# Three edits in a fused attention and feed-forward kernel: shifts of four heads turned at once, local values by tokens, reciprocals in PSUM

## The reference, cut to what matters

```
q, k, v = split_heads(x @ Wq), split_heads(x @ Wk), split_heads(x @ Wv)
# compressed branch: softmax over 32 blocks of 16 tokens (keys k_c, values v_c)
# selected branch: the 4 best blocks of each query, softmax over their 64 tokens
logits_s = where(allowed, einsum('bhtd,bhtnd->bhtn', q, k_s) / scale, NEG)
out_s = einsum('bhtn,bhtnd->bhtd', softmax(logits_s), v_s)
# local branch: the 33 last tokens of each query
wmask = (abs(pos[:, None] - pos[None, :]) <= WIN // 2) & (pos[:, None] >= pos[None, :])
out_l = einsum('bhts,bhsd->bhtd', softmax(where(wmask, q @ k.T / scale, NEG)), v)
out = gates[..., 0:1] * merge(out_c) + gates[..., 1:2] * merge(out_s) + gates[..., 2:3] * merge(out_l)
return out @ Wo
```

## Time and profile before

| | |
|---|---|
| time, median of 3 runs | 1504.34 us (1503.79 to 1508.48) |
| the profiled execution: its time | 1504.73 us |
| the profiled execution: its span, first to last instruction | 1503.0 us |
| TensorE busy | 1404.7 us (93%) |
| VectorE busy | 1213.4 us (81%) |
| ScalarE busy | 928.7 us (62%) |
| GpSimd busy | 918.6 us (61%) |
| mean granted clock of TensorE | 0.980 of full |

### The profile page before, as it was taken

How to read it: one execution, slowest core, us unless ns; L and a number is a source line. 1 busy time by engine, 2 the same in 40 slices (tenths; PEclk the granted TensorE clock), 3 DMA queues, 4 the chain that set the end, 5 groups by cost and what they waited for, 6 DMA issues and landing times. The chain is left out here.

```text
span 1503.0 us, 43856 instructions
## 1 busy us (share of the span) xinstructions
PE 1404.7 (93%) x14864; PEld 1045.2 (70%) x14960; DVE 1213.4 (81%) x4544; ACT 928.7 (62%) x1684; POOL 918.6 (61%) x845
## 2 busy tenths in 40 slices
PE   6899579999999999999999999999999999999978
PEld 4566437777777777777777777777777777777667
DVE  5545288888888889888888899999888888888812
ACT  3766336666666666666666666666666666666641
POOL 5655346666666666666666666666666666666620
PEclk8999869999999999999999999999999999999989
DMA  6556942221111222222111121222222222222027
GB/s 189 202 184 211 277 71 53 52 49 45 47 46 47 51 51 51 51 51 48 47 46 47 47 51 48 48 50 51 51 51 51 51 51 51 65 51 53 9 87 243
DMA packets 217147, 113.74 MB, mean 76 GB/s; under 512 B 128872, under 2 KB 211224, under 8 KB 217112
## 3 DMA queue, kind: packets, MB, share of 16 engines
q1 hardware_dynamic: 216304, 112.88, 27.5%
q10 hardware_dynamic: 808, 0.42, 0.2%
HBM read 73.08 MB, written 40.16 MB: 75 GB/s over the span
## 5 line engine op out<-in xcount | busy, mean ns | idle before, releaser
L1150 POOL TENSOR_TENSOR sumxy<-xy 128x1024 f32<-128x1024 f32 x128 | 240.7, 1900 | 0.0
L1393 DVE TENSOR_REDUCE bmax<-q_bank 128x32 f32<-128x512 f32 (+3 forms) x512 | 220.5, 483 | 19.9 <-PE q_bank L1633 19.7
L1240 ACT ACTIVATE pts<-k_bank 128x512 f32<-128x512 f32 (+2 forms) x384 | 177.7, 491 | 42.2 <-PE k_bank L1668 41.6
L1494 DVE SCALAR_TENSOR_TENSOR mw<-sumxy,c,ex 128x1024 f32<-128x1024 f32 x128 | 175.9, 1393 | 1.8 <-issue 1.0
L1633 PE MATMUL q_bank<-ko,qo 96*128 96x512 bf16 (+3 forms) x512 | 143.4, 307 | 26.0 <-DVE bmax L1393 24.7
L1116 POOL TENSOR_TENSOR pad<-pad 128x1 f32<-128x1 f32 x32 | 6.2, 194 | 256.5 <-DVE top L1412 256.5
L1615 PE MATMUL f_bank<-xt,wfu 128*128 128x128 f32 x1024 | 162.3, 281 | 0.0
L1174 POOL TENSOR_TENSOR cw<-cw,mw 128x1024 f32<-128x1024 f32 x64 | 150.8, 2357 | 8.1 <-ACT mw L1264 3.3
L1615 PE MATMUL f_bank<-xt,wfg 128*128 128x128 f32 x1024 | 150.5, 279 | 0.7 <-issue 0.7
L1615 PEld LDWEIGHTS f_bank<-xt,wfu 128*128 128x128 f32 x1024 | 139.4, 191 | 11.6
L1264 ACT ACTIVATE mw<-mw,erec 128x1024 f32<-128x1024 f32 x128 | 145.8, 1139 | 0.0
(11 more groups left out here) (211 smaller groups left out, 3373.6 us busy)
## 6 DMA issues: line engine op xcount, KB each, us to landing
qo<-s_qs SPq DMA_DIRECT2D x192, 64.0 KB, 2.2
ko<-s_ks SPq DMA_DIRECT2D x186, 64.0 KB, 2.2
s_qs<-parts SPq DMA_DIRECT2D x8, 768.0 KB, 4.9
s_ks<-parts SPq DMA_DIRECT2D x8, 768.0 KB, 6.3
s_v<-vo SPq DMA_DIRECT2D x8, 544.0 KB, 3.0
vv<-s_v SPq DMA_DIRECT2D x32, 136.0 KB, 2.3
vw<-s_v SPq DMA_DIRECT2D x64, 68.0 KB, 2.5
xin<-in_L_attn_x_dram SPq DMA_DIRECT2D x8, 512.0 KB, 7.2
```

The costliest lines, as they stand in the source:

```text
L1150: done("sum_done", g_.tensor_tensor(sumxy[:, h, :, :], xy[:, 0, h, 0:XK, None].broadcast_to([P, XK, KEYS]), xy[:, 1, h, None, :].broadcast ...
L1240: last = s.activation(pts[:, h, OFFS[j]:OFFS[j] + n], bank[:, 0:n], ACT.Exp)
L1393: last = v.tensor_reduce(bmax[:, i, h, 0:n], Q.bank(job)[:, o:o + n * BLK].rearrange("p (n j) -> p n j", j=BLK), AX.X, ALU.max)
L1494: done("mw_done", v.scalar_tensor_tensor(mw[:, h, :], sumxy[:, h, :, :].rearrange("p a b -> p (a b)"), c8[:, h, 7:8], ex[:, h % 2, :], ALU ...
```

## The change

1. **Shifts.** The rows for the shifts are no longer 96 to 127 of every head but rows 32h to 32h+31 of head h; the pair of parts that stood there stands in rows 96 to 127. So one `head_shifts(n)` turns all four heads with four matmuls (128 x 128 weights) into one K bank, job "a", and ScalarE copies it in four pieces of 32 rows. It runs inside the tail of step t, for n, between `token_values` and `experts_down(t, 1)`, and needs `shift_lo` and `shift_top` of n there. `queries` and `window` use all 128 rows, so the shift rows of `qo` must be zero until then: each load of parts first loads zeros there from a zero tensor in memory. With heads laid out differently, the loads of parts are 16 for keys and 16 + 4 for queries instead of 6 and 6. The lead gets the same, with the one-hot rows of `ko` copied by ScalarE's queue of transfers instead of GpSimd.
2. **Local values.** `local_values` swaps its operands: `pT` is the stationary one, and the output has tokens on the rows, 17 columns per tile and head. The transposition back (`tl`) and ScalarE's copy for it are gone. It is moved from step position (2,3) to behind `window(n)`, in two halves with the last part of mlp_down between them (which waits for the first half, `vl_half`). VectorE's `normalize(t, 1)` moves behind `local_scores(n)` and `selected_max(n)`.
3. **Reciprocals.** They are written back to the PSUM bank, so that the product with the gate has one operand in PSUM.
4. **Order on VectorE:** `expert_sum(t)` stands ahead of `key_marks(n)`.
5. **Last phase:** the first batch's `s_y` rows are loaded during the unit phase (`yr0`), and batch 1 waits only for its `ar` on TensorE.

```
-            k_jobs = ["pcT", "co", "a0"]
+            k_jobs = ["pcT", "co"]
             for h in range(HG):
-                k_jobs += [f"s{h}0", f"s{h}1", f"s{h}2"] + [f"a{h + 1}"] * (h < HG - 1) + [("pl0", "pl1", "vl", "tl")[h]]
-            k_jobs += ["vs", "ts"]
+                k_jobs += [f"s{h}0", f"s{h}1", f"s{h}2"] + [f"pl{h}"] * (h < 2)
+            k_jobs += ["vl", "vs", "ts", "a"]
...
+            PARTS = ((0, 0), (2, 0)), ((0, 1), (0, 2)), ((1, 0), (1, 1))
+            def part_rows(to, src, which, half):
+                for i, pair in enumerate(PARTS):
+                    lots = [(3, i, i + 1)] + [(i, h0, h1) for h0, h1 in ((0, i), (i + 1, HG)) if h0 < h1]
+                    for quad, h0, h1 in lots:
+                        for n in range(2):
+                            o = 32 * quad + D * n
+                            yield to[o:o + D, half, h0:h1, :], src[pair[n][which]][:, h0:h1, :]
...
-                    pairs = [(to[D * n:D * n + D, half, :, :], src[r])
-                             for to, src, parts in ((qo, q, Q_ROWS), (ko, k, K_ROWS))[:2 if keys else 1] for n, r in enumerate(parts)]
+                    pairs = [(qo[32 * h:32 * h + 32, half, h, :], s_zero) for h in range(HG)]
+                    pairs += part_rows(qo, q, 0, half)
+                    if keys:
+                        pairs += part_rows(ko, k, 1, half)
...
+                def head_shifts(t):            # ScalarE, at the end of step and lead
+                    K.wait_full(act, t, "a")
+                    for h in range(HG):
+                        rows = slice(32 * h, 32 * h + 32)
+                        last = s.activation(qo[rows, t.half, h, :], K.bank("a")[rows, :], ACT.Copy)
+                    K.released("a", last)
...
-                    cf.link(v.reciprocal(rs[:, :, :], bank[:, :, :, D]))
-                    cf.link(v.tensor_tensor(fs[:, :, :], rs[:, :, :],
+                    cf.link(v.reciprocal(bank[:, :, D], bank[:, :, D]))
+                    cf.link(v.tensor_tensor(fs[:, :, :], bank[:, :, D].rearrange("p (i h) -> p i h", i=TT),
...
+                def local_values(t, r):
+                    bank = K.bank("vl")
+                    rows = slice(64 * r, 64 * r + 64)
+                    for k in range(2):
+                        for g in range(T // 32):
+                            i, q = divmod(g, 4)
+                            o = VW * (HG * i + 2 * r + k)
+                            last = mm(bank[32 * q:32 * q + 32, o:o + VW], pT[rows, k, 32 * g:32 * g + 32],
+                                      vw[rows, t.half, g, VW * k:VW * k + VW], start=True, stop=True, skip_group_check=True)
...
+                def head_shifts(t):            # TensorE
+                    need(pe, "shift_lo", t)
+                    need(pe, "shift_top", t)
+                    K.wait_free(pe, t, "a")
                     for i in range(TT):
-                        last = mm(K.bank(f"a{h}")[SP3:P, P * i:P * i + P], shift_s[:, i, h, :], identb[:, :],
-                                  start=True, stop=True)
+                        last = mm(K.bank("a")[:, P * i:P * i + P], shift_s[:, i, :, :].rearrange("p h n -> p (h n)"),
+                                  identb[:, :], start=True, stop=True)
...
                     if n:
                         window(n, 0)
                         window(n, 1)
+                    local_values(t, 0)
+                    mlp_down(t, 3)
+                    local_values(t, 1)
                     selected_values(t)
                     transposed_weights(t)
                     experts_down(t, 0)
-                    token_values(t, 0)
+                    token_values(t)
+                    if n:
+                        head_shifts(n)
                     experts_down(t, 1)
```

More of the change, by code:

```diff
@@ L879, in build @@
         projecting.close()
+        sb, _, _ = make(outer)
+        yr0 = sb("yr0", [P, TT, C])
         inner = ExitStack()
@@ L1338, in step @@
                     shifts_and_blocks(t)
-                    openings(t)
+                    tanh(t, "g0", hidden(0), "th_done")
                     share(t, 2)
@@ L1572, in step @@
                             block_max(n, 1, part)
+                    expert_sum(t)
+                    if n:
                         key_marks(n)
@@ L1577, in step @@
                             block_max(n, 2, part)
-                    expert_sum(t)
                     if n:
@@ L1586, in step @@
                         block_shares(n)
-                    normalize(t, 1)
                     if n:
@@ L1693, in local_ready @@
                         K.wait_read(pe, t, f"pl{k}")
-                def local_values(t):
+                def local_values(t, r):
                     bank = K.bank("vl")
-                    for g in range(T // 32):
-                        for h in range(HG):
-                            rows, k = slice(64 * (h // 2), 64 * (h // 2) + 64), h % 2
-                            last = mm(bank[32 * h:32 * h + VW, 32 * g:32 * g + 32], vw[rows, t.half, g, VW * k:VW * k + VW],
-                                      pT[rows, k, 32 * g:32 * g + 32], start=True, stop=True, skip_group_check=True)
-                    K.filled("vl", last)
+                    rows = slice(64 * r, 64 * r + 64)
[5 more added lines that the diff above has]
+                                      vw[rows, t.half, g, VW * k:VW * k + VW], start=True, stop=True, skip_group_check=True)
+                    if r == 0:
+                        done("vl_half", last)
+                    else:
+                        K.filled("vl", last)
                 def local_shares(t, k):
@@ L1763, in mlp_down @@
                     for f in (2 * part, 2 * part + 1):
+                        if f == FT - 1:
+                            need(pe, "vl_half", t)
                         mm(Y.bank("y")[:, 0:C], hT[:, f, :], wfd[:, f, :], start=(f == 0), stop=False)
@@ L1790, in lead @@
                     window(n, 1)
-                    pe.wait_ge(key_blocks, 1)
+                    head_shifts(n)
                 def step(t):
@@ L1807, in step @@
                     up_rows(t, "g", 0, 1)
-                    head_shifts(t, 0)
                     up_rows(t, "g", 0, 2)
@@ L1845, in build @@
             ar = [ar0] + [sb(f"ar{b}", [P, TT, C]) for b in range(1, B)]
-            yr = [sb(f"yr{b}", [P, TT, C]) for b in range(B)]
+            yr = [yr0] + [sb(f"yr{b}", [P, TT, C]) for b in range(1, B)]
             aT = sb("aT", [P, 2, 2, T])
```

118 lines of the change are left out of this document (53 added, 65 removed).

## The result

The new kernel takes 1514.98 us (median of 4 runs, 1513.39 to 1520.06) against 1504.95 for the one before (4 runs, 1503.79 to 1508.48): a ratio of 1.0066, 95% interval 1.0041 to 1.0091. It is slower by two thirds of a per cent. The forecast was 1490.1 us, faster; the time lies inside the range (1473 to 1520) and on the other side of no change.

What follows compares the result with a forecast made beforehand. TensorE was taken as the bound, VectorE close behind; after the change GpSimd's chain would set the period at 38.45 us. From 1504.73: +2.5 - 12.3 - 1.8 - 2.6 = -14.2, so 1490.5, median 1490.1 us; range 1473 to 1520.

Steps and rivals of the forecast that it cites:

- What is late next: Section following GpSimd's chain round through the turning to the next step: period 38.45 us against 38.86, 12.3 us gained in 30.
- less 1.32 and 0.44 and plus 0.16 that is 35.49: TensorE's arrival at experts_down(t, 1), 37.09 us into the step, less head turnings and transposition, plus a local_values gap.
- 0.36 added for longer waits: TensorE's waits on block_max, 0.54 us a unit, grow by 0.36 at the last head, so it arrives at 35.85.
- TensorE's own work: Changes to turnings, transposition and local_values on TensorE sum to -1.25 us a unit, with nothing waiting.
- the two gaps of 0.16: Behind each half of local_values, a 0.16 us gap for draining the array; two instead of one.
- The chain of GpSimd: Third mw at 4.37 us, VectorE 16.30, handover 0.16, GpSimd 15.44 to shift_lo, then TensorE: period 38.45.
- Reciprocals: VectorE's product with the gate falls from 1.46 to about 0.2 us, but this gains nothing since yo waits for TensorE.
- Loads: SP's 36 loads of parts at pitch 0.466 land at 18.95 us, needed at 20.07: 1.1 us to spare.
- The lead: Turning shifts before w0 and more query transfers start step 1 at 255.4 instead of 252.93: +2.5 us.
- Last step and last phase: The last step saves 1.8 us, and the shorter wait for yr of batch 1 saves 2.6.
- The rivals named: TensorE decides, 1474.5 (0.17); SP's load queue, 1513 at pitch 0.52 (0.24); longer chain, 1499 to 1502 (0.13); local values, 1511 (0.05).
- the price of local values: Rival: local_values on TensorE at the upper end, +1.2 us a unit, of which waits cover 0.5: 1511; chance 0.05.

Runs made afterwards that it cites:

- at 40.8 and 37.2: Periods of two kernels: the new kernel with edit 4 undone, 1568.36 us, and the one with unsel on ScalarE, result_in late, zeros and mlp_down early, 1458.15 us.
- K1: The new kernel with unsel computed by ScalarE instead of VectorE: 1480.42 us, ratio 0.9845 to the kernel before.
- K5: K1 plus result_in late, zeros early, mlp_down parts 0 and 1 early, and block_shares late, added one by one: 1446.26 us, ratio 0.9606 to the kernel before.

## Why the prediction was wrong

**The step that failed** is TensorE's arrival at the turning in "What is late next": "less 1.32 and 0.44 and plus 0.16 that is 35.49", with 0.36 added for longer waits, 35.85. Measured 36.91. The sum takes work out of a whole step as if TensorE decided all of it. In the new kernel it decides only behind the window; ahead of it VectorE does, at 27.27 whether the turnings are there or not. What was taken out there (turnings 1.32, local values and the transposition 2.0, part 3 of mlp_down 1.1) is 4.4 us, and the window starts only 2.7 earlier (27.27 against 29.96): most of the rest turned into waits, on `block_max` 1.5 instead of 0.54, and 0.56 for `hT`, together 1.5 us more, where 0.36 was taken. And what was put behind it counts in full: 11.64 us to the next step instead of 8.86. So the unit comes out as long as before. That edit 2 moves work across the last wait was never priced; local values were priced for their size alone.

**A second price missed** is `unsel`. Edit 4 lets GpSimd's sums start 2.3 us earlier, and then they run under it: 1.97 instead of 0.42. The prediction priced contention with GpSimd for one product only, and did not ask which VectorE instruction the earlier sums would now meet. By the Trainium skill (SBUF — State Buffer, Who interferes with whom), not only a VectorE instruction with two inputs in SBUF contends with GpSimd: a `tensor_scalar`, as `unsel` is, can do so too when it runs in a 2-port mode. The trace agrees in the times (1.97 us under the sums, 0.42 without them); no view shows the mode. What it costs is known only in part: moving `unsel` from under the sums takes 0.23 us off the period, giving it to ScalarE takes 1.0 off, and other lengths change with either.

**Point by point.** TensorE's own work: -1.25 forecast, -1.26 measured, and that it fits to a hundredth is luck. Local values take 0.66 and 0.70, near the 1.4 taken, but the two gaps of 0.16 are not in the timeline, and the turning takes 0.22 instead of 0.35; with these the sum would be -1.7. Against it, the four parts of mlp_down take 0.3 more in the new order, and some matmul records are missing in both traces. The chain of GpSimd: third `mw` at +4.22 (4.37), `xy_in` to +20.5 (20.67), 15.60 on GpSimd (15.44), `shift_lo` at +36.2 (36.3): right to 0.2, but not what decides in the new kernel. It does in others: at 40.8 and 37.2, and with `unsel` earlier or on ScalarE. VectorE's wait ahead of `best_pairs` is gone and it waits ahead of `yo`: right. Reciprocals, worth nothing: right; the 0.2 for the product had no row behind it, and it took 0.17 us. Loads: no wait in the 28 units of the new kernel, some 1.1 to 1.5 us to spare against 1.1, though the pitch over all 36 is 0.486 and not 0.466: they land 1.7 us after issue instead of 2.2, and the unit is longer than forecast. Right by little: in step 1 TensorE does wait 1.33 us for them, and it waits in nearly every unit where local values stand in their old place. The lead: +2.5 forecast, step 1 starts 8.7 later. Of the 6.2 missed, 3.9 are there at the first load of the unit phase already (188.63 against 184.69); in the thirteen kernels with edit 1 that load comes at 184.7 to 188.8, in the three without it at 183.8 to 184.9, so most of the 3.9 is scatter between executions, and how much is edit 1's stays open. From that load to `w0` of step 0 it is 7.1 us more, where 6.1 was forecast: queries wait 4.5 us for `ko`, and 0.9 of a possible 6.5 was too low by 1.0. The wait of 4.75 at the turning was in the forecast's chain. Step 0 takes 40.37 instead of 39.05 (38.45 + 0.6), at a granted clock of 0.966, and not a lower one than before (0.943), as the 0.6 assumed. Last step and last phase: -4.4 forecast, -6.0 measured: 2.5 in the last step (1.8 forecast) and 3.5 in the last phase (2.6).

**The sum again.** Forecast +2.5 - 12.3 - 4.4 = -14.2; measured +8.7 + 3.9 - 6.0 + 2.1 = +8.7. The largest miss is the period (16.2 us), the next the lead and setup (6.2). Of the +3.9 in the periods 1.7 are step 1, with its wait for `ko`; the steady units were forecast 0.41 shorter and are 0.09 longer. The rivals named were not the cause there: neither loads nor the price of local values. "VectorE decides ahead of the window" was not among them.

**What stays open.** All twelve kernels with edits 1 and 2 together have 3.6 to 4.3 us outside the span, the four with at most one of the two 1.7 to 1.9. No view shows what those 2.1 us are. The scatter ahead of step 1 between executions, up to 4.0 us (258.1 to 262.1), is not explained either, nor is the length of step 1.

## What to carry to other kernels

When two engines hand work to and fro, mark for each stretch of the period which of them decides it; work taken out counts only where its own engine decides, and work moved from before the last wait to behind it is paid in full there and saves little where it stood. Ask of each edit that lets an engine start earlier under whose instructions it will now run. A wait that stays is a place for work from behind it: here half of the local values in another place were worth 22 us, and the five edits of K1 to K5 bring the kernel 3.9% below the one before the change. A wait put where another engine decides costs little, too: four more transfers made TensorE late in nearly every unit, and the units only 0.06 us longer.

## What the runs showed of the hardware

One VectorE instruction (`unsel`, input and output in SBUF, 512 elements a row, f32 to bf16) took 0.42 us in the three kernels where it stands clear of GpSimd's sums of 1024 elements, and 1.96 to 1.97 us in the mean in each of the eight where such a sum ran beside it. The same work took ScalarE 0.62 us, with GpSimd at work beside it. `bsel`, two inputs in SBUF, took from 0.69 to 2.35 us in the mean of a kernel, and GpSimd's `xb` 0.72 or 1.18; which of GpSimd's instructions makes which length was not separated. 64 small matmuls of 64 x 32 weights and 17 moving columns took 0.66 us, 10 ns each, where 128 of the old form took 1.40, 11 ns each.
